# Attention: the first half's maxima negated in slot 6, turned ahead of slot 8's scores, their row's transfers issued in slot 8

## What is computed

```python
qkv = x @ w_qkv.T + b_qkv
atten = softmax(einsum('bhqd,bhkd->bhqk', q, k) * SCALE)
out = einsum('bhqk,bhkd->bhqd', atten, v)
return out @ w_proj.T + b_proj
```

## Time and profile before

| what | value |
| --- | --- |
| median of 3 runs | 3131.01 us (3118.5 to 3137.04) |
| span of the profiled execution | 3169.6 us |
| attention, both layers | about 430 to 1870 us of the span |
| PE busy over the span | 87% |
| DVE, ACT, POOL busy over the span | 73%, 59%, 53% |
| DMA, mean | 125 GB/s |

### The profile page before, as it was taken

How to read it: one execution, slowest core, us unless ns; L and a number is a source line. 1 busy time by engine, 2 the same in 40 slices (tenths; PEclk the granted TensorE clock), 3 DMA queues, 4 the chain that set the end, 5 groups by cost and what they waited for, 6 DMA issues and landing times. The chain is left out here.

```text
span 3169.6 us, 95506 instructions
## 1 busy us (share of the span) xinstructions
PE 2756.1 (87%) x31491; PEld 2128.4 (67%) x31491; DVE 2320.9 (73%) x5326; ACT 1878.0 (59%) x3798; POOL 1671.7 (53%) x1957
## 2 busy tenths in 40 slices
PE   4999379998999988989998858988984999999998
PEld 3888345555555555555555538888874888888887
DVE  4888477887878787878787726766655777777776
ACT  3888256676666666666666637666642444444443
POOL 2777325455554666666666441556554444444444
PEclk8999688999999999999999969999986999999999
DMA  5564245667666666677767635444433444444443
GB/s 140 162 188 125 58 111 136 157 151 161 147 153 151 157 165 160 159 170 163 162 162 164 152 81 139 135 128 132 129 107 95 67 67 67 68 67 67 67 67 50
DMA packets 515433, 395.07 MB, mean 125 GB/s; under 512 B 223136, under 2 KB 488386, under 8 KB 515138
## 3 DMA queue, kind: packets, MB, share of 16 engines
q1 hardware_dynamic: 431426, 310.47, 40.2%
q0 software_dynamic: 38496, 46.38, 8.3%
q10 hardware_dynamic: 45216, 34.34, 4.6%
HBM read 232.59 MB, written 155.42 MB: 122 GB/s over the span
## 5 line engine op out<-in xcount | busy, mean ns | idle before, releaser
L701 DVE TENSOR_REDUCE a_mx<-a_mxp 98x4 f32<-98x784 f32 x768 | 747.5, 973 | 278.5 <-PE a_mxp L850 275.3
L540 ACT ACTIVATE a_pt<-a_st 98x784 f32<-98x784 f32 x768 | 633.9, 825 | 364.9 <-PE a_st L836 363.8
L1609 POOL DMA_INDIRECT out_dram<-f_yo,f_idg x202 | 329.8, 1633 | 417.2 <-DVE f_yo L1950 380.7
L481 POOL TENSOR_TENSOR a_cf<-a_ctxs,a_rec 128x1176 f32<-128x1176 f32 x64 | 171.5, 2680 | 456.1 <-DMA a_rec<-a_recip 456.1
L1687 ACT ACTIVATE f_hf<-f_bank,f_b1c 128x256 f32<-128x256 f32 x606 | 253.9, 472 | 236.5 <-PE f_bank L924 236.3
L865 PE MATMUL a_pv<-a_pt,a_vp 98*32 98x196 f32 x6144 | 359.6, 353 | 5.4 <-issue 4.4
L836 PE MATMUL a_st<-a_qst,a_kst 49*128 49x196 f16 x3072 | 268.1, 254 | 78.8 <-DMA a_qst<-a_mrow 54.2
L2112 PE MATMUL f_bank<-f_w2h,f_hh 128*128 x1212 | 298.9, 247 | 14.4 <-DVE f_hl L1934 13.0
L2113 PE MATMUL f_bank<-f_w2h,f_hl 128*128 x1212 | 298.2, 246 | 0.0
L2114 PE MATMUL f_bank<-f_w2l,f_hh 128*128 x1212 | 298.2, 246 | 0.0
L850 PE MATMUL a_mxp<-a_kst,a_qst 48*128 48x196 f16 x3072 | 264.9, 251 | 27.5 <-DVE a_mx L701 22.7
(11 more groups left out here) (324 smaller groups left out, 8367.6 us busy)
## 6 DMA issues: line engine op xcount, KB each, us to landing
a_rec<-a_recip SPq DMA_DIRECT2D x256, 147.0 KB, 4.9
t_rows<-in_x_dram SPq DMA_DIRECT2D x84, 392.0 KB, 5.9
a_qst<-a_qk SPq DMA_DIRECT2D x256, 110.2 KB, 3.1
a_kst<-a_qk SPq DMA_DIRECT2D x256, 110.2 KB, 3.8
f_xg<-f_listed SPq DMA_DIRECT2D x101, 264.0 KB
a_qk<-a_qkh SPq DMA_DIRECT2D x128, 196.0 KB, 3.1
a_qk<-a_qkl SPq DMA_DIRECT2D x128, 98.0 KB, 3.4
a_qk<-a_qkh SPq DMA_DIRECT2D x128, 98.0 KB, 2.5
```

The costliest lines, as they stand in the source:

```text
L540: act.activation(pt[k % PT][:].rearrange("p j a t -> p j (a t)"), st_ps[0:half_t, :, 0:unit_t], ACT.Exp, scale=sm_scale).then_inc(exp_s, 1)
L701: dve.tensor_reduce(mx[:, a, :, 2 * p:2 * p + 2].rearrange("p q j -> p j q"), mx_ps[0:half_t, :, 0:unit_t].rearrange("p j (q t) -> p j q t ...
L1609: pool.indirect_dma_start(out, bass.IndirectOffsetOnAxis(ap=idg[i % 3][:, t:t + 1], axis=0), yo[i % 3][:, t, :], None, compute_op=ALU.add) ...
```

## The change

The maxima of the first half of unit s+1 take their way from DVE to `qst` earlier. `NEGATED_AT` goes from 7 to 6. `turn_maxima(s+1, 0)` goes from the end of slot 8 to its start. The weighted sum of slot 8 changes sides with it: it stood ahead of slot 8's scores, and now stands behind the scores and the turned scores, and waits there for ACT's copy of the maxima row (a wait that the weighted sum of slot 10 had before). On ACT, `maxima_row` moves ahead of slot 8's exponential, `place_maxima` right behind it, and the context copy of slot 8 behind that; the issue of `xres` keeps its line and so comes behind all three.

```diff
-        ROWS_FIRST, PART_FIRST, CONTEXT_FIRST, VALUES_FIRST = (1, 1, 1), (0, 0), (0, 1, 1, 0, 0, 1), (0, 0)
-        NEGATED_AT, RECIP_AT, STATS_AT, AGGREGATE_AT = 7, 5, (9, 1), 4
+        ROWS_FIRST, PART_FIRST, CONTEXT_FIRST, VALUES_FIRST = (1, 1, 1), (0, 0), (0, 1, 0, 0, 0, 1), (0, 0)
+        NEGATED_AT, RECIP_AT, STATS_AT, AGGREGATE_AT = 6, 5, (9, 1), 4
...
                 for k in range(SLOTS):
                     empty(k, 1)
+                    if k == MAXIMA_AT[1] and "M" in kinds:
+                        maxima_row(s + 1, 0)
                     if "C" in kinds:
...
+                    if k == MAXIMA_AT[1] and "M" in kinds:
+                        place_maxima(s + 1, (par + 1) % 2, 0)
                     empty(k, 0)
...
-                    if k == 9 and "M" in kinds:
-                        place_maxima(s + 1, (par + 1) % 2, 0)
                     if k == MAXIMA_AT[0] and "C" in kinds:
                         maxima_row(s, 1)
-                    if k == MAXIMA_AT[1] and "M" in kinds:
-                        maxima_row(s + 1, 0)
...
-                    if k in (4, 6, 8, 10) and "C" in kinds:
-                        weighted_sums(s, par, k // 2 - 2, 2 * s + 2 if k == 4 else 2 * s + 3 if k == 10 and "M" in kinds else None)
+                    if k == MAXIMA_AT[1] and "M" in kinds:
+                        turn_maxima(s + 1, 0)
+                    if k in (4, 6, 10) and "C" in kinds:
+                        weighted_sums(s, par, k // 2 - 2, 2 * s + 2 if k == 4 else None)
...
                         turned_scores(s + 1, (par + 1) % 2, k - 1)
+                    if k == 8 and "C" in kinds:
+                        weighted_sums(s, par, 2, 2 * s + 3 if "M" in kinds else None)
...
-                    if k == MAXIMA_AT[1] and "M" in kinds:
-                        turn_maxima(s + 1, 0)
...
-                wait(pe, ctx_s, GROUPS * u if a else GROUPS * (u - 1) + 3)
+                wait(pe, ctx_s, GROUPS * u if a else GROUPS * (u - 1) + 2)
```

## The result

| | before | after |
| --- | --- | --- |
| median | 3131.01 us | 3148.72 us |
| lowest to highest, 9 runs each | 3118.5 to 3147.01 | 3139.22 to 3159.51 |
| span of the profiled execution | 3169.6 us | 3149.1 us |

The ratio on record is 1.0076 [1.0052, 1.0101]: the change makes the kernel 0.8% slower, 24 us, where the prediction had 0.35% faster. The two medians of the table lie 17.7 us apart, 1.0057, inside that interval, so the loss is best read as 18 to 24 us. The time lies in the given range, at its upper end, and on the wrong side.

The account below looks back on a forecast made before the run. PE's 0.89 us wait a step for the maxima row was the target, beside a reciprocal loop as long as the step. First layer -14 us, second +3, together -11: 3131 to 3120 us, range 3092 to 3150.

Parts of the forecast that it names:

- ACT's two issues: ACT between slots 8 and 9: 1.4 us of issuing is covered; slot 11's scores come 0.42 us later through PE's work.
- What is late next: Loops after the change: first-layer steps shorten by about 0.45 us, second-layer steps lengthen by 0.1; together -11 us.
- The row's transfers: Maxima row, issued 2.0 us earlier and ahead of xres: PE's wait ahead of slot 0's scores goes, -54.2 us gross.
- D: Rival: the row stays late behind the broadcast's packets, PE keeps about half the wait; 3130 us, chance 0.21 together with C.
- The weighted sum of slot 8: PE in slot 8: 0.84 us lies uncovered, PE idles 0.50 us ahead of the scores, query rows start 0.50 later.
- PE's gross gain: PE over 61 steps: the removed wait of 54.2 us less 0.42 us a step, 28.6 us.
- reciprocal loop: From reciprocal through broadcast, POOL and cn to the next reciprocal: 19.07 + 2.80 us, as long as the 21.87 us step.
- The negation: DVE, moved to slot 6: delays the reciprocal loop by 0 to 0.5 us, taken as 0.1.
- `xres` behind the broadcast: Transfer queues: the broadcast of the reciprocals lands 0 to 1.3 us earlier, taken as 0.6.
- rival B: The sums loop closes the step in both layers, so only slot 11's lateness counts: +18 to +26 us, chance 0.15.
- A: Rival: all of PE's gain arrives, with some 10 us more in the second layer; 3092 to 3102 us, chance 0.22.
- C: Rival: PE's wait moves whole from the row to cn; 0 to +5 us, chance 0.21 together with D.

Follow-up runs that it names:

- filled pair: The changed kernel and the kernel before, each with 16 unread matmuls added in PE's slot 2: ratios 1.0015 and 1.0006.
- a_noneg_xres_first: The changed kernel without negation on DVE and with xres issued ahead of the row's transfers: ratio 1.0023 to the kernel before.
- b_noneg: The kernel before without negation on DVE; PE turns the raw maxima by a constant matmul instead: ratio 1.0012.
- a_xres11: The changed kernel with xres issued in slot 11: ratio 1.0065 to the kernel before.
- b_neg6: The kernel before with only the first half's negation moved, from slot 7 to slot 6: ratio 1.0003.
- a_noneg: The changed kernel without negation on DVE; PE turns the raw maxima by a constant matmul instead: ratio 0.9954 to the kernel before.
- b_xres11: The kernel before with xres issued in slot 11 instead of slot 8: ratio 1.0102.
- filled partner: The kernel before with xres issued in slot 11 and 16 unread matmuls added in PE's slot 2: ratio 0.988.
- b_fill: The kernel before with 16 unread matmuls added in PE's idle stretch in slot 2: ratio 1.0006.
- a_xres_first_fill: The changed kernel with xres issued ahead of the row's transfers and 16 unread matmuls in PE's slot 2: ratio 1.0044 to the kernel before.
- a_fill: The changed kernel with 16 unread matmuls added in PE's idle stretch in slot 2: ratio 1.0015 to the kernel before.
- a_xres_first: The changed kernel with xres issued right behind slot 8's exponential, ahead of the row's transfers: 3140.41 us, ratio 1.0073 to the kernel before.
- b_xres_late: The kernel before with xres issued in slot 9, behind the row's transfers, instead of slot 8: ratio 0.9998.

## Why the prediction was wrong

The forecast was -11 us, the loss is 18 to 24. Two steps of the prediction failed. "ACT's two issues" called them covered between slots 8 and 9; with the context copy and `xres` in the same gap they weren't, and slot 11's scores came 0.86 us later, not 0.42. And "What is late next" took POOL's earlier start as pure gain; in the runs it lengthened the negation of slot 0, PE paused, and its clock fell in more steps. The filled pair says that the second is most of the loss.

- *The row's transfers: right.* The wait of 54.2 us is gone, in all steps, and D with it. But its removal was worth nothing: a_noneg_xres_first is no faster than b_noneg without it.
- *The weighted sum of slot 8: right.* 0.48 us idle ahead of slot 8's scores for 0.50, and slot 9's scores at 6.23 for 6.14.
- *ACT's two issues: the step that failed first.* "Between slots 8 and 9 the same 1.4 us end at 647.7, and the next thing ACT must do, the query rows, is not ready before 648.3: covered." The 1.4 us are not alone in that gap. I moved the issue of `xres` behind them in the part on the broadcast and left it, and the context copy, out of this sum. The cover was 0.6 us (647.7 to 648.3), and the two take 0.35 + 0.32 = 0.67: it was used up, with nothing for the pauses between ACT's instructions. Those are what came on top: the issues ended 0.14 us later behind slot 8's scores than forecast (1.92 us for 1.78), the copy started 0.11 behind them, the pass 0.25 behind `xres`. So slot 9's exponential starts 0.96 us behind its scores; in the step of before it is 648.36 - 647.77 = 0.59. The difference, 0.37, is slot 10's (8.07 for 7.61, with the 0.09 of slot 9). Slot 11's scores came 0.86 us later, not 0.42, and 61 times 0.86 is 52 us: PE's gross gain was 2 us, not 28.6. a_xres11, with `xres` elsewhere, has about the forecast's size, 0.53 and 0.29.
- *The reciprocal loop "at zero to spare": not shown.* 19.07 + 2.80 is the step's length by construction, since the 2.80 are what is left up to the next reciprocal. What speaks for a tight loop is PE's wait for `cn`, and it is 0.29 us in that step and 6.3 us in 20 of the 61 steps:

```profile
661.26 0.28 PE L924 MATMUL a_pr<-a_pl,a_ones 128*98 128x192 f16 x1 [0.29 <-POOL a_cn L485]
```

- *The negation: right in its new place* (b_neg6), and the wrong one to look at. The prediction quotes the row that mattered, the negation at 655.44 that took 1.07 us and ended with POOL's instruction, and uses it as a measure for slot 6. It didn't ask what happens to this row when POOL starts sooner, which the next item of the same text forecast: the row lengthened from 0.77 us on average over all steps to 1.12.
- *`xres` behind the broadcast: right in kind, too small.* Taken 0.6, at most 1.3; measured 1.07 and 1.80 us. The bound, 294 KB at the mean rate of ACT's queue, was too low; why it gives more isn't settled. As a gain it was real: without the lock it is worth 0.7% (a_noneg against a_noneg_xres_first).
- *What is late next: the step that cost most.* Missing from the list, and so put at nothing: TensorE's clock. What takes over from the wait is none of the loops but the pause of PE that POOL's earlier start makes by way of DVE, 1.26 us in the step shown. The clock of the timed runs says how much of it there is. Of 3149 us at a mean of 0.947, 2 x 0.053 x 3149 = 334 us are at the low level; of 3131 at 0.954, 288. The change adds 46 us at the low level. Work done in 46 us at half speed takes 23 at full, so by this estimate it costs 23 us at most, and 17 at the rate of b_xres11 and its filled partner (407 - 222 = 185 us less at the low level, 1.0102 - 0.988 = 69 us less time: 0.37 each). The rate isn't one for all kernels: b_fill has less time at the low level than before and is no faster. The firmer figure is the filled pair: 0.76% unfilled, 0.09% filled, which leaves 21 us of the 24 to the clock.
- *The rest* is 0.1% by the filled pair. It is two things that nearly cancel: the later slot 11, +0.4% (a_xres_first_fill against b_fill), and the earlier broadcast, -0.3% (a_fill against a_xres_first_fill). The first shows in the second layer, whose steps at full clock went from 22.17 in before to 22.52 us in after; that the sums do it is argued, from 18 waits for them in some 23 steps where there were 12. The later slot 11 is rival B's mechanism: with the scores 0.86 us late, twice what B had, it is worth 12 us, under B's 18 to 26, and in the first layer it isn't seen: the steps at full clock are 21.92 and 21.96. That the result, 3148.72, meets the near end of B's 3149 to 3157, and so the end of the range that was set by it, is luck: the reason is mostly not B's.
- *A and C.* A fell with slot 11: no gain at PE came through. C fell as well; PE's wait for `cn` became shorter (6.3 to 3.2 us), not longer as forecast.

One thing is not settled. a_xres_first loses 0.7% with POOL's start where before has it. Its clock, 0.950, lies 0.004 below before's, some 26 us at the low level and 10 to 13 us of time, which is the half of its loss that the fill gives back. Its profiled execution has 10 steps at the low clock, as before's, and 81 us at the low level from the first reciprocal to the last, for 82. So what lowers its clock in the timed runs isn't in the one trace that there is, and no run here tells it. It also means that putting POOL's start back doesn't by itself bring the time back: that start is the source of the long negations in after, but not the only way to lose 0.7%.

## What to carry to other kernels

When an instruction is moved on an engine, add up all that stands in the gap it goes to, the issues of transfers too: each takes its time from the next computing instruction (0.68 us for one of the row here), even if its data isn't urgent. When something starts sooner, look for rows of other engines whose duration depends on it: a 0.2 us instruction that waits out another engine's is visible in the trace of before as one whose duration varies with no change of shape. And read the granted clock for each kernel compared: in b_xres11, 1.10 us of useless matmuls in PE's pause were worth 2.2%, and in before nothing.

## What the runs showed of the hardware

- VectorE's TENSOR_SCALAR of 98x24 took 0.17 us with POOL idle and what POOL's TENSOR_TENSOR had left otherwise, up to 2.15 us in after. Under POOL's TENSOR_SCALAR pieces, four in 1.97 us, 47 of them took 0.27 us on average and 0.46 at most: the negation of slot 6 meets only these pieces, and stays cheap.
- A pause of PE of 1.26 us, with PE busy 0.51 of 1.70 us, was followed by about 7 us at the 1.2 GHz level, with PE busy all through. In after 16 of 26 negations over 1.2 us were followed by such a stretch. With the pause filled, nearly all are gone (24 to 1 or 2 steps in b_xres11), and a fill of 1.10 us cost the steps at full clock 0.26 to 0.30 us in before and after, and nothing in b_xres11 (first layer).
- The order of issue on two queues moved the landing of a broadcast by more than the later transfer's own mean share: 294 KB moved behind it brought the landing forward by 1.1 to 1.8 us in after and by 2.1 in b_xres_late.
